# Keys and values of one attention layer projected side by side, with one context row per partition

## The chip, the cores and the metric

The kernel runs on one core of a Trainium2 chip. The metric is the device time of one execution in microseconds. A core has a matrix engine (PE, with its weight loads PEld), a vector engine (DVE), a scalar engine (ACT), a general engine (POOL), and a queue (SP) that issues the DMAs. Each engine runs its own instructions in order and waits on semaphores for the others.

## The reference

Eight stages are added to a residual `x` of 2 x 256 tokens by 512: four cross-attention layers and four small feed-forward layers. The fourth attention layer, `L3_xattn`, is the one that the change touches. It has 32 query heads in 8 groups of 4, one key and one value head of width 128 for each group, and 2 x 512 context rows:

```
q = rmsnorm(x @ Wq.T, q_norm_w)
k = rmsnorm(ctx @ Wk.T, k_norm_w)      # over the 128 values of a row; weight per value
v = ctx @ Wv.T
out = softmax(q @ k.T / sqrt(128) + mask) @ v @ Wo.T
```

Everything is float32. To keep the precision each operand is split in a high part (rounded to the matrix engine's fast float32 form) and a low part (the rest), and each product is three matmuls: high x high, high x low, low x high.

## The kernel before, in words

The four attention layers share one code (`attn_tensor`, `attn_vector`, `attn_scalar`, `attn_gpsimd`), with a table `ATTN` of what stands where. `walk` goes over the groups: two heads straight, then a loop that holds two groups in its body and starts at the third head (heads 2 and 3 of one group, heads 0 and 1 of the next, and so twice), then the rest straight. In the fourth layer the loop's body runs three times, so the loop's end is taken back twice.

A group has 4 heads and each head 4 slots, one for each tile of 128 queries. A slot is written (head, tile). In each slot the engines do the following for a tile:

- PE: `scores` of the tile two slots ahead (3 matmuls into `psS`), `transposes` of this tile's probabilities (4 into `psT`), in tiles 0 and 2 half of the weighted values (`weighted_v`, 12 matmuls of 256 columns into `psO`), in one slot of each head the query projection (12 matmuls into `psQ`), and then the units that the table `prep` or `outs` names.
- DVE: `row_max` of the tile two ahead (scale and mask L891, maximum L895), `pT_low` (L909), `row_recip` (L905), in tile 0 the low part of the output (`o_low`, L931), the low part of the query, then its share of the units.
- ACT: `pT_high`, `row_exp`, in tile 0 `o_high`, the query's high part, its share of the units, and the high parts of weights.
- POOL: `norm` (L1202), its share of the units, and the low parts of weights.

A unit uses one of two banks of `psX`, in turn. A unit may start on PE when the unit two before it has been read out, which DVE signals by `x_free`, in the order of the units. The units that `prep` names make keys and values for the next group:

- `k0`, `k1` (PE L369, 12 matmuls of 512 columns each): keys of one batch, with the 128 values of a key on the partitions and the 512 rows as columns. ACT squares them into `ksq` (L1124), DVE stores them times the norm's weight in `scr` (L966).
- `m0`, `m1` (PE L810): the sum of squares over the partitions, 4 products with a column of ones. DVE scales (L968), POOL takes the power -0.5 into `k_r` (L1219) and spreads it on diagonals (L1223).
- `b0`, `b1` (PE L814): a product of ones with these diagonals, so that every partition has every row's factor. DVE multiplies the keys by it (L970), ACT rounds them (L1131), DVE takes the low part (`k_low`, L937).
- `v0`, `v1` (PE L369, 12 matmuls of 512 columns): values in the same layout; DVE copies them to `scr` (L976). `t0`, `t1` (PE L805): 4 transposes each, since the weighted sum needs a row of values per partition. ACT rounds (L1143), DVE takes the low part (L979).
- `q` (PE L819) does for a query head what `m` does for the keys, in tile 0 of each head; DVE (L982) and POOL (L1228) follow.

`out` (PE L369, 12 matmuls of 512 columns) adds the previous group's output to `x` in slots (0,1), (0,2), (0,3) and (1,0).

## Time and profile before

| | |
|---|---|
| median of 3 runs | 2156.29 us (2155.64 to 2157.31) |
| the profiled execution, its time | 2155.29 us |
| its span, first to last instruction | 2153.5 us |
| mean granted TensorE clock | 0.968 |
| PE busy | 1971.2 us (92%) |
| PEld / DVE / ACT / POOL busy | 77% / 69% / 48% / 44% |
| chain that ended last | PE 64%, DVE 18%, ACT 9%, issue 7% |

```profile
PE   5999999999748999998988999997799999999997
DVE  5777787777777887887334555656467766677676
PEclk9999999999978999999988999999899999999999
```

These strips cut the span in 40 slices of 53.8 us; a digit is the busy share in tenths, and for the last row the granted clock. The fourth attention layer starts with a query projection at 1533 us, in slice 29, and ends at about 2120 us. The profile gives a matmul's duration with its pipeline depth, so two matmuls that follow each other overlap; what a matmul costs PE is the distance from its start to the next one's start. "[0.32 <-ACT x L1]" at a row's end is the idle time before the instruction and what ended it.

### The profile page before, as it was taken

Reading aid. Unit: us, or ns where it says so; the run is one execution under the profiler, and the core shown is the slowest. Engines: PE = TensorE matmul, PEld = TensorE weight load, DVE = VectorE, ACT = ScalarE, POOL = GpSimd, SP = SyncE. Lnnn points to the kernel's source line nnn. Section 1 sums busy time; section 2 is a strip of 40 time slices with the busy share of each in tenths; the row PEclk is TensorE's granted clock in tenths of the full one; section 3 lists DMA queues with packets and bytes.
Section 4 is the critical chain, followed back from the end, with each engine's and each line's share of the span. In section 5 each row is a group of like instructions: output and inputs, shape, how many; then the busy total and the mean of one; then the engine's idle time right before and its main releaser. Section 6 shows DMA issues by size and latency. Waiting matters only on the chain.

```text
span 2153.5 us, 33307 instructions
## 1 busy us (share of the span) xinstructions
PE 1971.2 (92%) x10874; PEld 1651.7 (77%) x10874; DVE 1475.5 (69%) x2725; ACT 1029.6 (48%) x2264; POOL 938.5 (44%) x971
## 2 busy tenths in 40 slices
PE   5999999999748999998988999997799999999997
PEld 4788888888636888887666888886678888888886
DVE  5777787777777887887334555656467766677676
ACT  3666666666514544553123544542155555545552
POOL 2555554554445665664321323322144444444432
PEclk9999999999978999999988999999899999999999
DMA  3222221122211111111210101001101110111001
GB/s 140 57 64 75 77 85 57 61 74 67 92 34 40 63 65 54 52 45 64 67 54 4 34 8 34 23 1 55 54 11 47 47 46 11 50 45 45 14 23 45
DMA packets 47070, 106.77 MB, mean 50 GB/s; under 512 B 6065, under 2 KB 21937, under 8 KB 43105
## 3 DMA queue, kind: packets, MB, share of 16 engines
q1 hardware_dynamic: 46944, 105.14, 15.3%
q8 instruction: 74, 1.21, 0.2%
q14 instruction: 52, 0.42, 0.1%
HBM read 98.37 MB, written 6.75 MB: 49 GB/s over the span
## 4 chain that ended last, share of the span: by engine, by line
PE 64%; DVE 18%; ACT 9%; issue 7%; POOL 1%; DVEq 0%; ACTq 0%; POOLq 0%
PE psX L369 23%; PE psQ L369 11%; PE psS L369 11%; PE psO L369 10%; PE psT L752 5%; DVE pT_lo L909 2%; ACT pT_hi L1092 1%; DVE dq_space L461 1%; DVE nmax L897 1%; ACT dq_space L448 1%; DVE p_sb L891 1%; DVE nbias L895 1%; PE psT L369 1%; ACT p_sb L1085 1%; DVE qscr L470 1%
## 5 line engine op out<-in xcount | busy, mean ns | idle before, releaser
L1202 POOL TENSOR_SCALAR p_sb<-p_sb,rrec 128x512 f32<-128x512 f32 (+1 forms) x320 | 266.0, 831 | 704.1 <-DVE rrec L905 704.0
L1092 ACT ACTIVATE pT_hi<-psT 128x512 fp32r<-128x512 f32 (+2 forms) x384 | 235.0, 612 | 336.9 <-PE psT L752 336.0
L909 DVE TENSOR_TENSOR pT_lo<-psT,pT_hi 128x512 fp32r<-128x512 f32 (+2 forms) x384 | 271.4, 707 | 81.9 <-ACT pT_hi L1092 81.9
L369 PE MATMUL psO<-pT_hi,v_hi 128*128 128x256 f32 (+1 forms) x832 | 255.1, 307 | 41.0 <-DVE pT_lo L909 34.1
L752 PE MATMUL psT<-ident,p_sb 128*128 128x128 f32 x1600 | 243.3, 277 | 13.9 <-POOL p_sb L1202 10.5
L369 PE MATMUL psO<-pT_hi,v_lo 128*128 128x256 f32 (+1 forms) x832 | 237.0, 285 | 0.0
L369 PE MATMUL psO<-pT_lo,v_hi 128*128 128x256 f32 (+1 forms) x832 | 237.0, 285 | 0.0
L752 PEld LDWEIGHTS psT<-ident,p_sb 128*128 128x128 f32 x1600 | 195.9, 142 | 53.1 <-POOL p_sb L1202 15.8
L369 PE MATMUL psQ<-xnT_hi,wq_hi 128*128 128x512 f32 (+1 forms) x448 | 189.0, 422 | 18.7 <-DVE qscr L869 9.2
L1085 ACT ACTIVATE p_sb<-psS,nbias 128x512 f32<-128x512 f32 (+1 forms) x192 | 145.3, 757 | 126.6 <-DVE nbias L899 126.6
L369 PEld LDWEIGHTS psO<-pT_hi,v_hi 128*128 128x128 f32 (+1 forms) x832 | 155.0, 186 | 54.2 <-DVE pT_lo L909 45.9
L369 PE MATMUL psS<-kT_hi,q_hi 128*128 128x512 f32 (+2 forms) x448 | 176.8, 395 | 20.4 <-ACT p_sb L1085 18.7
L369 PE MATMUL psQ<-xnT_hi,wq_lo 128*128 128x512 f32 (+1 forms) x448 | 180.2, 402 | 0.0
L369 PE MATMUL psQ<-xnT_lo,wq_hi 128*128 128x512 f32 (+1 forms) x448 | 179.7, 401 | 0.0
L369 PE MATMUL psX<-wo_hi,oT_hi 128*128 128x512 f32 (+1 forms) x432 | 173.1, 401 | 0.0
L369 PE MATMUL psX<-wo_hi,oT_lo 128*128 128x512 f32 (+1 forms) x432 | 169.8, 393 | 0.0
L369 PE MATMUL psX<-wo_lo,oT_hi 128*128 128x512 f32 (+1 forms) x432 | 169.5, 392 | 0.0
L624 POOL TENSOR_TENSOR wq_lo<-wq_f,wq_hi 128x512 fp32r<-128x512 f32 (+1 forms) x112 | 141.5, 1264 | 59.1 <-ACT wq_hi L612 59.1
L897 DVE TENSOR_REDUCE nmax<-psS 128x1 f32<-128x512 f32 (+1 forms) x192 | 148.1, 772 | 23.4 <-PE psS L369 23.3
L369 PE MATMUL psS<-kT_lo,q_hi 128*128 128x512 f32 (+2 forms) x448 | 163.6, 365 | 0.0
L369 PE MATMUL psS<-kT_hi,q_lo 128*128 128x512 f32 (+2 forms) x448 | 163.3, 364 | 0.0
L369 PE MATMUL psX<-cT_hi,wkv_hi 128*128 128x512 f32 (+1 forms) x384 | 157.6, 410 | 0.8 <-DVE q_ms L982 0.2
(337 smaller groups left out, 4786.2 us busy)
## 6 DMA issues: line engine op xcount, KB each, us to landing
wq_f<-in_a_wq SPq DMA_DIRECT2D x96, 256.0 KB, 2.7
wo_f<-in_a_wo SPq DMA_DIRECT2D x24, 1024.0 KB, 6.1
wkv_f<-in_a_wkv SPq DMA_DIRECT2D x24, 512.0 KB, 3.9
mask_sb<-in_codes SPq DMA_DIRECT2D x32, 174.0 KB, 2.4
qscr<-in_amax SPq DMA_DIRECT2D x32, 174.0 KB, 2.3
w<-qscr SPq DMA_DIRECT2D x32, 174.0 KB, 1.9
wo_f<-in_f_wT SPq DMA_DIRECT2D x3, 1024.0 KB, 5.2
wq_f<-in_a_wq SPq DMA_DIRECT2D x16, 192.0 KB, 2.3
```

Of the source, the lines that this page charges most:

```text
L369: mm = pe.matmul(dst, w, m, start=(first and k == 0), stop=(last and k == n - 1))
L448: ins = act.activation(tiles[q], dq_codes[h % 2], ACT.Copy, scale=slope, bias=NF4[c] - slope * c)
L461: dve.tensor_tensor(t[0], t[0], t[2], ALU.min).then_inc(dq_low, 1)
L470: dve.tensor_tensor(t[0], t[0], t[2], ALU.max).then_inc(dq_high, 1)
L624: L.wq_lo.inc(pool.tensor_tensor(lo, f, hi.bitcast(F32), ALU.subtract))
L752: mm = pe.transpose(t_view(L, j)[:, i, :], p_view(L, j, h)[:, m * P:(m + 1) * P], ident[:, :])
L891: L.s_mask.inc(dve.scalar_tensor_tensor(p_view(L, j), s_view(L, j)[:, 0:L.open(j)], scale, mask_sb[:, t * L.keys:t * L.keys + L.open(j)], ...
L897: L.s_nm.inc(dve.tensor_reduce(nmax[:, j:j + 1], s_view(L, j), AX.X, ALU.max, negate=True))
L909: L.t_lo.inc(dve.tensor_tensor(pT_view(L, pT_lo, j), t_view(L, j), pT_view(L, pT_hi, j).bitcast(F32), ALU.subtract))
L1085: L.s_exp.inc(act.activation(p_view(L, j), src, ACT.Exp, bias=nbias[:, j:j + 1], scale=1.0 if L.masked else L.scale, accum_out=rsum[:, j:j ...
L1092: L.t_hi.inc(act.activation(pT_view(L, pT_hi, j), t_view(L, j), ACT.Copy))
L1202: L.s_norm.inc(pool.tensor_scalar(p_view(L, j), p_view(L, j), rrec[:, j:j + 1], 1.0, ALU.mult, ALU.mult))
```

## The change

In the fourth layer the weights of keys and values are interleaved in memory, so that for each 128 inputs 128 columns of keys and 128 of values lie side by side (`wkv_rows`). The context is now the stationary operand and the weights are streamed. The units of the layer become:

- `n0` to `n3`: each takes two tiles of 128 context rows. PE does 24 matmuls of 256 columns; a bank holds two halves of 128 key values and 128 values, with a context row per partition. ACT squares the two key tiles with the sum accumulated in the same instruction (into `k_ms`), then writes `v_hi`. DVE writes `v_lo`. POOL does a small scaling and the power -0.5 on 2 columns (L1246, L1248 of the changed kernel). DVE multiplies the keys by the factor into `scr` (`k_scale`), and only this frees the bank.
- `k0`, `k1`: 4 transposes each of these keys. ACT and DVE write the high and low parts with the norm's weight, straight from `psX`.

`m`, `b`, `v`, `t` and `k_low` are gone. `k_scale` of a unit stands on DVE in the slot after the unit's, behind `row_max`, `pT_low`, `row_recip` and `o_low`; for `n0` in slot (1,3), the last before the loop's end, it stands at the end of the same slot. `k0` is behind `n1` and `k1` behind `n3` by an explicit wait, and every unit is behind the unit two before it.

```diff
          outs=OUT_EARLY, splits=SPLIT_TILES,
-         prep={(1, 3): ["k0"], (2, 0): ["k1", "m0"], (2, 1): ["m1"], (2, 2): ["b0"], (2, 3): ["v0", "b1"],
-               (3, 0): ["t0"], (3, 1): ["v1"], (3, 2): ["t1"]}),
+         prep={(1, 3): ["n0"], (2, 2): ["n1"], (2, 3): ["n2"], (3, 0): ["k0"], (3, 1): ["n3"], (3, 2): ["k1"]}),
...
-        diag = rows[:, :].rearrange("p (a b) -> p a b", b=P)
+        ksq_tiles = ksq[:, :, :].rearrange("p a (t d) -> p (a t) d", d=P)
+        kn = scr[:, :, :].rearrange("p a (t d) -> p (a t) d", d=P)
+        wkv_rows = [z[:, :, :].rearrange("p a (c n) -> p (a c) n", n=2 * P) for z in (wkv_hi, wkv_lo)]
...
                     if h == 0:
-                        if L.masked:
+                        if L.rope:
                             L.k_lo.wait(pe, g.at(L.n_k, L.n_k))
-                        else:
+                        elif not L.rms:
                             prev = g.to(-1) if g.off else None
                             L.x_free.wait(pe, L.use(prev, f"k{L.n_k - 1}")[0] + 1)
+                if L.rms and h == 0 and j in (0, 2):
+                    prev = g.to(-1) if g.off else None
+                    L.x_free.wait(pe, L.use(prev, f"k{b}")[0] + 1)
...
+                elif kind == "n":
+                    L.wkv_lo.wait(pe, gp.at(2, 2))
+                    for z in (0, 1):
+                        at = (2 * i + z) * P
+                        mm = three(pe, X[:, z * 2 * P:(z + 1) * 2 * P],
+                                   [([m[:, c, at:at + P] for m in (cT_hi, cT_lo)], [w[:, c, :] for w in wkv_rows])
+                                    for c in range(DC)])
+                elif kind == "k" and L.rms:
+                    L.x_free.wait(pe, L.use(g, f"n{2 * i + 1}")[0] + 1)
+                    for m in range(4):
+                        mm = pe.transpose(X[:, m * P:(m + 1) * P], kn[:, 4 * i + m, :], ident[:, :])
...
-                elif kind == "m":
-                    L.k_f.wait(pe, L.count(g, "k", f"k{i}"))
-                    for m in range(4):
-                        mm = pe.matmul(X[:, m:m + 1], ksq[:, i, m * P:(m + 1) * P], ones[:, 0:1],
-                                       start=True, stop=True)
-                elif kind == "b":
-                    L.k_diag.wait(pe, L.count(g, "b", what))
-                    mm = pe.matmul(X, ones[:, :], diag[:, :, :].rearrange("p a b -> p (a b)"), start=True, stop=True)
...
-                    ins = dve.tensor_scalar(scr[:, i, :], X, vecs[:, 1:2], None, ALU.mult)
-                elif kind == "m":
-                    ins = dve.tensor_scalar(k_ms[:, i, :], X[:, 0:4], 1.0 / hd, EPS, ALU.mult, ALU.add)
-                elif kind == "b":
-                    ins = dve.tensor_tensor(scr[:, i, :], scr[:, i, :], X, ALU.mult)
-                    late.append((g, i, kpar))
+                    ins = dve.scalar_tensor_tensor(k_lo, X, vecs[:, 1:2], k_hi.bitcast(F32), ALU.mult, ALU.subtract)
+                elif kind == "n":
+                    c = slice(2 * i * P, 2 * (i + 1) * P)
+                    dve.tensor_tensor(v_lo[:, kpar, c].rearrange("p (t d) -> p t d", d=P), halves(X)[:, :, P:2 * P],
+                                      v_hi[:, kpar, c].bitcast(F32).rearrange("p (t d) -> p t d", d=P), ALU.subtract)
+                    late.append((g, what, X))
+                    return
...
+            def k_scale(g, what, X):
+                i = int(what[1])
+                L.k_r.wait(dve, 2 * (i + 1) if g is None else g.at(8, 8 + 2 * (i + 1)))
+                L.x_free.inc(dve.tensor_tensor(kn[:, 2 * i:2 * i + 2, :], halves(X)[:, :, 0:P],
+                                               k_r[:, i // 2, 2 * (i % 2):2 * (i % 2) + 2].unsqueeze(2).broadcast_to([P, 2, P]),
+                                               ALU.mult))
...
+                    while L.rms and late:
+                        k_scale(*late.pop(0))
...
-                    while late and late[0] in before:
-                        k_low(*late.pop(0))
+                    while L.rms and late and (h, j) == (1, 3):
+                        k_scale(*late.pop(0))
...
-                if kind == "k" and L.rms:
+                if kind == "n":
                     L.x_mm.wait(act, k + 1)
-                    L.k_f.inc(act.activation(ksq[:, i, :], X, ACT.Square))
-                elif (kind == "k" and L.rope) or kind == "b":
-
-                    if L.rope:
-                        L.k_f.wait(act, L.count(g, "k", what))
-                    else:
-                        L.x_free.wait(act, k + 1)
+                    for z in (0, 1):
+                        t = 2 * i + z
+                        ins = act.activation(ksq_tiles[:, t, :], halves(X)[:, z, 0:P], ACT.Square,
+                                             accum_out=k_ms[:, t // 4, t % 4:t % 4 + 1])
+                    L.k_sq.inc(ins)
+                    c = slice(2 * i * P, 2 * (i + 1) * P)
+                    L.x_act.inc(act.activation(v_hi[:, gp.par, c].rearrange("p (t d) -> p t d", d=P),
+                                               halves(X)[:, :, P:2 * P], ACT.Copy))
...
+                    elif L.rms:
+                        ins = act.activation(dst, X, ACT.Copy, scale=vecs[:, 1:2])
...
-                elif what[0] == "m":
+                elif what[0] == "n":
                     i = int(what[1])
-                    L.x_free.wait(pool, k + 1)
-                    L.k_r.inc(pool.tensor_tensor(k_r[:, i, :], k_ms[:, i, :], half[:, 0:4], ALU.pow))
-                    L.k_r.wait(pool, L.count(g, "m", what))
-                    if i:
-                        L.x_mm.wait(pool, L.use(g, "b0")[0] + 1)
-                    L.k_diag.inc(pool.tensor_tensor(diag[:, :, :], ident[:, :].unsqueeze(1).broadcast_to([P, 4, P]),
-                                                    k_r[:, i, :].unsqueeze(2).broadcast_to([P, 4, P]), ALU.mult))
+                    at = (slice(None), i // 2, slice(2 * (i % 2), 2 * (i % 2) + 2))
+                    L.k_sq.wait(pool, i + 1 if g is None else g.at(4, 4 + i + 1))
+                    pool.sem_inc(wait_met, 1)
+                    L.k_r.inc(pool.tensor_scalar(k_ms[at], k_ms[at], 1.0 / L.hd, EPS, ALU.mult, ALU.add))
+                    L.k_r.wait(pool, 2 * i + 1 if g is None else g.at(8, 8 + 2 * i + 1))
+                    L.k_r.inc(pool.tensor_tensor(k_r[at], k_ms[at], half[:, 0:2], ALU.pow))
...
-        k, v = (split(w, n).reshape(n, P, DC * hd) for w in (wk, wv))
-        arrays[f"a{i}_wkv"] = np.stack([k, v], axis=2)
+        k, v = (split(w, n).reshape(n, P, DC, hd) for w in (wk, wv))
+        arrays[f"a{i}_wkv"] = np.stack([k, v], axis=3 if i == 3 else 2).reshape(n, P, 2, DC * hd)
```

On DVE, at slot (3,0), from its `row_max` on, before (L891 mask, L895 maximum, L909 `pT_low`, L905 `row_recip`, L931 `o_low`, L982 and L979 the reads of `q` and `t0`, L937 `k_low`):

```order
L891 SCALAR_TENSOR_TENSOR p_sb<-psS,q_r,mask_sb 128x512
L125 REGISTER_ALU
L895 TENSOR_REDUCE nbias<-p_sb 128x1
L909 TENSOR_TENSOR pT_lo<-psT,pT_hi 128x4x128
L905 RECIPROCAL rrec<-rsum 128x1
L125 REGISTER_ALU
L931 TENSOR_TENSOR oT_lo<-psO,oT_hi 128x512
L125 REGISTER_ALU
L982 TENSOR_SCALAR q_ms<-psX 128x4
L125 REGISTER_ALU
L979 TENSOR_TENSOR v_lo<-psX,v_hi 128x512
L937 TENSOR_TENSOR kT_lo<-scr,kT_hi 128x512
```

and after, one `v_lo` (L977, of `n2`) earlier (L902, L906, L920, L916 and L942 are the same five steps, L997 is `k_scale`):

```order
L977 TENSOR_TENSOR v_lo<-psX,v_hi 128x256
L124 REGISTER_ALU
L902 SCALAR_TENSOR_TENSOR p_sb<-psS,q_r,mask_sb 128x512
L124 REGISTER_ALU
L906 TENSOR_REDUCE nbias<-p_sb 128x1
L920 TENSOR_TENSOR pT_lo<-psT,pT_hi 128x4x128
L916 RECIPROCAL rrec<-rsum 128x1
L124 REGISTER_ALU
L942 TENSOR_TENSOR oT_lo<-psO,oT_hi 128x512
L124 REGISTER_ALU
L997 TENSOR_TENSOR scr<-psX,k_r 128x256
L124 REGISTER_ALU
```

The bank of `n2` is freed by the row L997, which stands behind the five steps; `k0` on PE needs that bank.

On DVE, at slot (3,2), the same; before, from the end of slot (3,1), with the copy of `v1` (L976) that frees its bank ahead of the next `row_max`:

```order
L905 RECIPROCAL rrec<-rsum 128x1
L125 REGISTER_ALU
L976 COPY scr<-psX 128x512
L125 REGISTER_ALU x2
L891 SCALAR_TENSOR_TENSOR p_sb<-psS,q_r,mask_sb 128x512
L125 REGISTER_ALU
L895 TENSOR_REDUCE nbias<-p_sb 128x1
L909 TENSOR_TENSOR pT_lo<-psT,pT_hi 128x4x128
L905 RECIPROCAL rrec<-rsum 128x1
L125 REGISTER_ALU
L979 TENSOR_TENSOR v_lo<-psX,v_hi 128x512
```

and after, from the read of `n3` (L977) on:

```order
L977 TENSOR_TENSOR v_lo<-psX,v_hi 128x256
L124 REGISTER_ALU x2
L902 SCALAR_TENSOR_TENSOR p_sb<-psS,q_r,mask_sb 128x512
L124 REGISTER_ALU
L906 TENSOR_REDUCE nbias<-p_sb 128x1
L920 TENSOR_TENSOR pT_lo<-psT,pT_hi 128x4x128
L916 RECIPROCAL rrec<-rsum 128x1
L124 REGISTER_ALU
L997 TENSOR_TENSOR scr<-psX,k_r 128x256
L124 REGISTER_ALU
L974 SCALAR_TENSOR_TENSOR kT_lo<-psX,vecs,kT_hi 128x512
```

The row that frees `n3` moved from ahead of the four steps of slot (3,2) to behind them; PE's `k1` is in this slot.

On PE, at the end of slot (2,1), before:

```order
L369 MATMUL psQ<-xnT_lo,wq_hi 128x512
L125 REGISTER_ALU x2
L810 MATMUL psX<-ones,xn_f 128x1 x4
L125 REGISTER_ALU
L369 MATMUL psS<-kT_hi,q_hi 128x512
L369 MATMUL psS<-kT_hi,q_lo 128x512
L369 MATMUL psS<-kT_lo,q_hi 128x512
```

and after:

```order
L371 MATMUL psQ<-xnT_lo,wq_hi 128x512
L124 REGISTER_ALU
L371 MATMUL psS<-kT_hi,q_hi 128x512
L371 MATMUL psS<-kT_hi,q_lo 128x512
L371 MATMUL psS<-kT_lo,q_hi 128x512
```

The sum over partitions is gone, and `psS` follows the projection directly.

## Rows read from the trace of the kernel before

**Rows 1.** First line of the page.
```profile
span 2153.5 us, 33307 instructions
```

**Rows 2.** Busy time by stretch, fourth layer's loop: start:end, length, engines, clock, DMA, GB/s.
```profile
1600.00:2080.00 480.00, 476.12 (x2767) 407.45 (x2766) 340.05 (x620) 244.97 (x508) 216.12 (x228) 1.00 0.12 37
```

**Rows 3.** PE in time, end of `m0`: start, us, engine, line, work.
```profile
1672.57 0.95 PE L810 MATMUL psX<-ones,xn_f 128*128 128x1 f32 x8
...
1673.38 0.49 PE L369 MATMUL psS<-kT_hi,q_hi 128*128 128x512 f32 x1
...
1673.71 0.40 PE L369 MATMUL psS<-kT_hi,q_lo 128*128 128x512 f32 x1
```

**Rows 4.** PE in time, around `b0`.
```profile
1680.82 1.02 PE L814 MATMUL psX<-rows,ones 128*128 128x512 f32 x2
...
1681.28 0.79 PE L369 MATMUL psS<-kT_hi,q_hi 128*128 128x512 f32 x1
...
1681.91 0.39 PE L369 MATMUL psS<-kT_hi,q_lo 128*128 128x512 f32 x1
```

**Rows 5.** Chain of waits, one projection unit: start, us, what.
```profile
1663.76 2.77 PE psX L369 x12
```

**Rows 6.** Groups by form, PE, 1600 to 2080 us: busy us, mean ns, idle before.
```profile
L810 PE MATMUL psX<-ones,xn_f 128*128 128x1 f32 x112 | 13.4, 241 | 3.2 <-DVE q_ms L982 3.2
...
L805 PE MATMUL psX<-ident,scr 128*128 128x128 f32 x56 | 8.6, 277 | 0.0
```

**Rows 7.** PE in time, slot (3,2) from its scores to `t1`.
```profile
1694.51 0.39 PE L369 MATMUL psS<-kT_hi,q_hi 128*128 128x512 f32 x1
...
1695.75 0.28 PE L369 MATMUL psO<-pT_hi,v_lo 128*128 128x256 f32 x1
...
1697.05 0.60 PE L805 MATMUL psX<-ident,scr 128*128 128x128 f32 x4
```

**Rows 8.** DVE in time, steps of slots (3,0) and (3,1).
```profile
1690.35 0.16 DVE L905 RECIPROCAL rrec<-rsum 128x1 f32<-128x1 f32 x1 [0.28 <-ACT p_sb L1085]
...
1690.83 0.69 DVE L931 TENSOR_TENSOR oT_lo<-psO,oT_hi 128x512 fp32r<-128x512 f32 x1 [0.32 <-ACT oT_hi L1114]
...
1693.04 0.75 DVE L891 SCALAR_TENSOR_TENSOR p_sb<-psS,q_r,mask_sb 128x512 f32<-128x512 f32 x1
...
1695.39 0.16 DVE L905 RECIPROCAL rrec<-rsum 128x1 f32<-128x1 f32 x1 [0.29 <-ACT p_sb L1085]
```

**Rows 9.** Groups by form, ACT, whole run.
```profile
L1081 ACT ACTIVATE p_sb<-p_sb,nbias 128x128 f32<-128x128 f32 x64 | 25.7, 402 | 81.4 <-DVE nbias L885 81.4
...
L1085 ACT ACTIVATION_READ_ACCUMULATOR p_sb<-p_sb,nbias 128x1 f32 x128 | 23.8, 186 | 0.0
```

**Rows 10.** Groups by form, DVE, whole run: a 128x256 product.
```profile
L1594 DVE TENSOR_TENSOR xn_f<-xn_f 128x256 f32<-128x256 f32 x1 | 0.4, 426 | 0.0
```

**Rows 11.** Groups by form, POOL, whole run.
```profile
L1219 POOL TENSOR_TENSOR k_r<-k_ms,half 128x4 f32<-128x4 f32 x16 | 16.2, 1013 | 26.2 <-DVE k_ms L968 26.2
```

**Rows 12.** DVE in time, across the loop's end.
```profile
1738.05 0.75 DVE L966 TENSOR_SCALAR scr<-psX,vecs 128x512 f32<-128x512 f32 x1 [0.32 <-ACT xn_f L1124]
...
1741.44 0.75 DVE L891 SCALAR_TENSOR_TENSOR p_sb<-psS,q_r,mask_sb 128x512 f32<-128x512 f32 x1 [2.63 <-issue]
...
1744.88 0.15 DVE L982 TENSOR_SCALAR q_ms<-psX 128x4 f32<-128x4 f32 x1
```

**Rows 13.** PE in time, `m0` after the loop's end.
```profile
1745.16 1.05 PE L810 MATMUL psX<-ones,xn_f 128*128 128x1 f32 x8 [1.39 <-DVE q_ms L982]
```

**Rows 14.** PE in time, start of the layer: first `k0`, then the second query projection.
```profile
1537.51 0.39 PE L369 MATMUL psX<-cT_hi,wkv_hi 128*128 128x512 f32 x1
...
1559.23 0.48 PE L369 MATMUL psQ<-xnT_hi,wq_hi 128*128 128x512 f32 x1
```

**Rows 15.** PE in time, a wait near the end of the third layer.
```profile
1433.97 0.63 PE L369 MATMUL psS<-kT_hi,q_hi 96*128 96x512 f32 x1 [2.43 <-ACT p_sb L1085]
```

**Rows 16.** Busy time by stretch, after that wait.
```profile
1433.00:1440.00 7.00, 6.03 (x33) 5.66 (x34) 3.07 (x6) 3.13 (x6) 2.64 (x3) 0.76 0.00 0
```

More of the change, by code:

```diff
@@ L371, in three, with halves @@
             return mm
+        def halves(bank):
+            return bank.rearrange("p (t n) -> p t n", n=2 * P)
         def flat(t):
@@ L1029, in head @@
                         row_recip(*settled)
-                    before = list(late)
                     while L.rope and late:
@@ L1209, in use @@
             def use(g, what):
-                if what[0] not in "kmq" or what[0] == "out":
+                if what[0] not in "knq" or what[0] == "out":
                     return
```

30 lines of the change are left out of this document (16 added, 14 removed).

## The prediction

> **What bounds the kernel now.** I read the page's span first [rows 1], then the busy time by stretch: over 480 us of the fourth layer's loop PE is busy 476 us at granted clock 1.00, that is at 2.4 GHz, and DVE, ACT and POOL are busy 71%, 51% and 45% [rows 2]. So in this layer time is PE's work plus the little it waits. Then I read PE in order of time, because a matmul's duration overlaps the next; only distances between starts count. Last I read DVE in order of time, since DVE frees the banks that PE's units wait for. PE never waited for the value transposes `t` (idle 0.0) and 3.2 us in all for `m` [rows 6], the whole of it after the loop's end. The group row also gives the count: 112 records at 8 for each `m` are 14 units, two for each of the 7 groups that prepare a next one.
>
> **PE's work.** A unit `m` takes 0.81 us from its start to the scores behind it, and the first matmul of these takes 0.33 us instead of 0.23, because it follows work in the other float form [rows 3]: 0.91 us. A unit `b` takes 0.46 us, and the matmul behind it 0.63 instead of 0.23 [rows 4]: 0.86 us. Two of each go: 3.54 us for a group. A `k` or `v` unit of 12 matmuls of 512 columns takes 2.77 us [rows 5]; the weighted values show what 256 columns with a weight load each cost, 11 in 1.30 us, 0.118 us each [rows 7]. An `n` unit of 24 is then 2.84 us, and four cost 0.28 us more than the four units that they replace. The new `k` transposes are as many as the `t` ones were, in the same slots, so they cancel. Net -3.26 us for a group, -22.8 us for 7.
>
> **A wait that the change adds at `k1`.** I count from the start of slot (3,2) on PE, which is the end of `n3`. PE reaches the transposes after 1697.05 - 1694.51 = 2.54 us [rows 7]. `k1` needs `k_scale` of `n3`. Before that, ACT squares two tiles of 128 columns, each with the read of its sum. Nothing shows this form; the nearest is an exponential of 128 columns at 0.40 us with a read of 0.19 us behind it [rows 9]. An activation starts about 0.1 us before the last one's end, so that two squares hold ACT 0.8 us by this row; from below I put 0.55 us, an estimate, a third less for a form that takes no bias operand. Copying the values to `v_hi` takes 0.4 to 0.5 us (the same row's 0.40 us is for half the columns). With 0.2 us until the last product has landed and a semaphore passed, DVE can start on `v_lo` at 1.2 to 1.5 us, and holds 0.35 us for it (a 128x256 product lasts 0.43 us [rows 10]). Then `row_max`, the maximum, `pT_low` and the reciprocal stand in front: from a mask's start to a reciprocal's start 1695.39 - 1693.04 = 2.35 us, and 0.16 us for it [rows 8]. Then `k_scale`, 0.43 us. The sum is 4.5 to 4.8 us against PE's 2.54: a wait of 2.0 to 2.3 us. I take 2.2. Behind it on PE's queue stand the scores of the next head and the query projection, so it is paid in full.
>
> **And at `k0`.** In slot (3,0) PE does scores, transposes, half of the weighted values and the `q` unit, 3.4 us: the 2.54 us above holds the first three, and the `q` sum is as long as an `m`, 0.81 us. `k0` follows `n2` by two units and needs its bank. DVE's chain is the same, with `o_low` in it, which starts 1690.83 - 1690.35 = 0.48 us after the reciprocal and holds DVE 0.6 us [rows 8]. `k_scale` ends at 5.5 to 5.8 us: a wait of 2.1 to 2.4 us. I take 2.3. The two waits are 4.5 us for a group and 31.5 us for 7, more than PE's saved work. As ends for the pair I keep 2.8 us for a group (each square nearly free, and `v_lo` let through before ACT has finished other work) and 5.5 us (the new small instructions are as long as their nearest rows).
>
> **POOL and the loop's end.** POOL's scaling of 2 columns has no row; the power on 4 columns lasts 1.01 us [rows 11]. I take 0.35 us and 0.9 us, with 0.1 us and 1.0 us as the ends for the first. This is hidden where `k_scale` stands a slot later, since the factor is there before DVE comes to it. In slot (1,3) it isn't hidden: `k_scale` of `n0` stands at the slot's end and waits for POOL. There DVE's last instruction started at 1738.05, 0.75 us after PE's slot, and the loop's end cost 3.39 us from there to the next one [rows 12]. Now the last is `k_scale`, which starts after squares (0.9 us), scaling and power and POOL's `norm` before them, at about 2.6 us. DVE enters the loop's body 1.9 us later than before, near 1743.3 on the old time axis. PE has lost its `m` and `k1` units in (2,0) and (2,1), so it comes early: it waits about 1.4 us at the transposes of slot (2,2), whose probabilities come from that late `row_max`, and 1.8 us more at the weighted values behind them, which need `pT_low` of slot (2,1), itself behind the `q_ms` that was at 1744.88 [rows 12]. In place of this, the old wait of 1.39 us at `m0` [rows 13] goes. Net +1.6 us, twice: +3.2 us. In the groups without a loop's end a small part of this remains, some 0.3 us in 5 groups, +1.5 us.
>
> **The layer's start.** From the first key unit to the second query projection it was 1559.23 - 1537.51 = 21.7 us [rows 14], with waits and a lowered clock in it. The new chain is: `n0` and `n1` 5.7 us, `n2` to 8.8, `k0` to 9.2, a wait for `n2` to be read until 11.8, `n3` to 14.6, a wait of 3 us, `k1` and `q` to 18.8. That is 2.9 us less, and the two waits of nearly 3 us will cost part of it by the clock: I take -1 us, between -3 and +2.
>
> **Clock.** After a wait of 2.43 us [rows 15] seven microseconds had a mean clock of 0.76 [rows 16], with part of the stretch at 1.2 GHz; 0.24 x 7 = 1.7 us were lost. Behind the 1.39 us of [rows 13] the loop's mean of 1.00 [rows 2] shows no such loss. The new waits of 2.2 us lie between. I put one fall, +2 us, in the sum. The Trainium skill, "TensorE: Matmul & The Clock Gate", section "HAM oscillation — how this bites in real kernels", says that the array's clock is halved again after idle gaps, and that a kernel with such a gap in each tile pays each time. By that rule the sum would be that of the second rival below. The trace agrees for one gap of 2.43 us and shows none for the short ones.
>
> **Sum.** -22.8 + 31.5 + 3.2 + 1.5 - 1 + 2 = +14.4 us on the profiled execution's 2155.3 us (its span of 2153.5 and 1.8 us around it) gives 2169.7. The median is 1.0 us above that execution: 2170.7, so I say 2171 us.
>
> **Rivals.**
> 1. Faster: the waits don't appear, because DVE, idle 29% of the loop [rows 2], runs far enough ahead of PE that each bank is free in time. For it speaks that `t` never waited [rows 6]; against it, that the copy which freed `v1` stood ahead of `row_max`, and `k_scale` stands behind it, and that the scores of this `row_max` are themselves made by PE at the slot's start, so DVE can't run ahead. Then 2156.3 - 22.8, and 2.9 us less at the start: 2131 us. It decides if the waits of a group stay below 3.3 us.
> 2. Slower still: the clock falls at most of the 14 long waits. For it [rows 15, 16], against it the short stretch of each wait. 10 falls at 1.7 us instead of 1: 2171 + 15 = 2186 us.
> 3. No change: the mechanism holds, but both waits are near their low end, 2.8 us for a group: 12 us less, 2159 us.
> 4. The weight loads of the `n` units don't hide behind 256 columns, so that each matmul takes as long as one weight load. The loop's loads are 407.45 / 2766 = 0.147 us long on average [rows 2]; 96 matmuls at that instead of 0.118 us are 2.8 us for a group, and 2171 + 8 x 2.8 = 2193 us. The weighted values do the same pattern at 0.118 us [rows 7], so I hardly believe it.
>
> **How the numbers follow.** The forecast has 0.60, the faster rival 0.11, the clock 0.14, no change 0.12, weight loads 0.03. The point is the forecast's. The forecast's own range, from waits of 3.5 to 5.3 us for a group and the start's bounds, is 2162 to 2179 us. The range 2151 to 2187 us takes in the third rival and the second, and leaves out the first and the fourth and the ends, about 0.2. What a measurement of this kernel can tell from no change is about 0.2%, 4.3 us: faster 0.11, within it 0.13, slower 0.76.
>
> **What would show it.** In the changed kernel's groups of work: no `m` or `b`; `n` matmuls 0.118 us apart; PE idle before the transposes of `scr` of about 4.5 us for a group, with DVE's `scr` as releaser, split evenly on `k0` and `k1`; PE waits at `psT` and `psO` just behind the loop's end; a loop body of two groups 2 x (4.5 - 3.26) + 0.3 + 1.6 = 4.4 us longer than before. If the transposes show idle under 3 us for a group, my chain on DVE is wrong; if the `n` matmuls are further apart than 0.13 us, the PE term is.

## The result

| | median | runs |
|---|---|---|
| before | 2156.80 us | 4 (2155.64 to 2158.45) |
| after | 2168.69 us | 4 (2166.28 to 2171.01) |

The ratio is 1.0056, with a 95% interval from 1.0041 to 1.0070: the change makes the kernel 12 us slower. The profiled execution of after took 2167.1 us, 11.8 us more than that of before.

### The profile page after: what moved, and what is told of

It reads as the page before. It is cut to its first block, busy times and chain, and to the rows that moved or that the text cites. A ratio compares the mean times of both kernels' runs of the same rounds, so it can differ in the third digit from the quotient of the medians.

```text
span 2165.3 us, 33868 instructions
## 1 busy us (share of the span) xinstructions
PE 1956.6 (90%) x11098; PEld 1660.2 (77%) x11098; DVE 1451.2 (67%) x2709; ACT 1042.6 (48%) x2392; POOL 933.5 (43%) x1003
## 4 chain that ended last, share of the span: by engine, by line
PE 63%; DVE 17%; ACT 9%; issue 7%; POOL 1%; DVEq 0%; ACTq 0%; POOLq 0%
PE psX L371 24%; PE psQ L371 11%; PE psS L371 10%; PE psO L371 9%; PE psT L760 5%; DVE pT_lo L920 2%; ACT pT_hi L1111 1%; DVE dq_space L466 1%; ACT dq_space L453 1%; DVE nmax L908 1%; DVE p_sb L902 1%; ACT p_sb L1104 1%; PE psT L371 1%; DVE nbias L906 1%; DVE qscr L475 1%
## 5 line engine op out<-in xcount | busy, mean ns | idle before, releaser
L920 DVE TENSOR_TENSOR pT_lo<-psT,pT_hi 128x512 fp32r<-128x512 f32 (+2 forms) x384 | 271.1, 706 | 82.3 <-ACT pT_hi L1111 82.3
L371 PE MATMUL psS<-kT_hi,q_hi 128*128 128x512 f32 (+2 forms) x448 | 171.0, 382 | 24.3 <-ACT p_sb L1104 18.7
L1104 ACT ACTIVATE p_sb<-p_sb,nbias 128x512 f32<-128x512 f32 x128 | 92.6, 724 | 136.2 <-DVE nbias L906 136.1
```

Of the source, the lines that this page charges most:

```text
L371: mm = pe.matmul(dst, w, m, start=(first and k == 0), stop=(last and k == n - 1))
L920: L.t_lo.inc(dve.tensor_tensor(pT_view(L, pT_lo, j), t_view(L, j), pT_view(L, pT_hi, j).bitcast(F32), ALU.subtract))
L1104: L.s_exp.inc(act.activation(p_view(L, j), src, ACT.Exp, bias=nbias[:, j:j + 1], scale=1.0 if L.masked else L.scale, accum_out=rsum[:, j:j ...
```

## The profile after

The first line of the page, against [rows 1]:

```profile
span 2165.3 us, 33868 instructions
```

The busy time of the loop's stretch (start:end, length, then PE, PEld, DVE, ACT, POOL, the granted clock, the share of the DMA engines and GB/s), against [rows 2]:

```profile
1600.00:2080.00 480.00, 449.69 (x2890) 402.30 (x2891) 313.08 (x596) 253.57 (x611) 206.92 (x252) 0.99 0.12 37
```

PE is busy 449.69 us of 480, where it was 476.12. DVE and POOL are less busy than before, and ACT only 9 us more, so no engine took PE's place as the bound. PE waits. For what, the groups by form show (busy us, mean ns, idle before), against [rows 6]:

```profile
L371 PE MATMUL psX<-wkv_hi,cT_hi 128*128 128x256 f32 x216 | 63.6, 294 | 0.0
L371 PE MATMUL psO<-pT_hi,v_hi 128*128 128x256 f32 x208 | 62.4, 300 | 1.6 <-DVE pT_lo L920 1.6
...
L806 PE MATMUL psX<-ident,scr 128*128 128x128 f32 x56 | 10.1, 307 | 24.8 <-DVE scr L997 24.8
```

L806 are the transposes of `k0` and `k1`: 24.8 us of idle time, all released by DVE's `scr`, the result of `k_scale`. 56 records at 4 for each unit are 14 units. In the order of time each `k0` waits 1.86 or 1.87 us and each `k1` 1.66 to 1.68 us (1.73 once, in the last group). Here is PE in slot (3,2) of one group, in the order of time, with what stood there before in [rows 7]:

```profile
1843.81 0.40 PE L371 MATMUL psS<-kT_hi,q_hi 128*128 128x512 f32 x1
...
1846.25 0.28 PE L371 MATMUL psO<-pT_lo,v_hi 128*128 128x256 f32 x1
1848.20 0.66 PE L806 MATMUL psX<-ident,scr 128*128 128x128 f32 x4 [1.68 <-DVE scr L997]
```

And DVE in the same slot, against [rows 8]:

```profile
1844.94 0.42 DVE L977 TENSOR_TENSOR v_lo<-psX,v_hi 128x256 fp32r<-128x256 f32 x1 [1.04 <-ACT v_hi L1149]
1845.28 0.74 DVE L902 SCALAR_TENSOR_TENSOR p_sb<-psS,q_r,mask_sb 128x512 f32<-128x512 f32 x1
1846.06 0.69 DVE L906 TENSOR_REDUCE nbias<-p_sb 128x1 f32<-128x512 f32 x1
1846.66 0.68 DVE L920 TENSOR_TENSOR pT_lo<-psT,pT_hi 128x512 fp32r<-128x512 f32 x1
1847.62 0.16 DVE L916 RECIPROCAL rrec<-rsum 128x1 f32<-128x1 f32 x1 [0.29 <-ACT p_sb L1104]
1847.72 0.42 DVE L997 TENSOR_TENSOR scr<-psX,k_r 128x256 f32<-128x256 f32 x1
```

From the mask step (L902) to `k_scale` (L997) it is 2.44 us from start to start, in which DVE waits for ACT (0.29 us on the reciprocal), and the transposes on PE begin 0.06 us after the end of `k_scale`. ACT, which starts the chain, was quicker than predicted; the same view of ACT, against [rows 9]:

```profile
1844.01 0.28 ACT L1145 ACTIVATE xn_f<-psX 128x128 f32<-128x128 f32 x1 [0.30 <-PE psX L371]
1844.18 0.20 ACT L1145 ACTIVATION_READ_ACCUMULATOR xn_f<-psX 128x1 f32 x1
1844.27 0.27 ACT L1145 ACTIVATE xn_f<-psX 128x128 f32<-128x128 f32 x1
1844.43 0.20 ACT L1145 ACTIVATION_READ_ACCUMULATOR xn_f<-psX 128x1 f32 x1
1844.52 0.38 ACT L1149 ACTIVATE v_hi<-psX 128x256 fp32r<-128x256 f32 x1
```

The two squares with their reads hold ACT from 1844.01 to 1844.52, 0.51 us. POOL's two instructions, groups by form over 1600 to 2080 us, against [rows 11]:

```profile
L1248 POOL TENSOR_TENSOR k_r<-k_ms,half 128x2 f32<-128x2 f32 x27 | 19.0, 703 | 2.2
...
L1246 POOL TENSOR_SCALAR k_ms<-k_ms 128x2 f32<-128x2 f32 x27 | 5.2, 193 | 6.2 <-ACT xn_f L1145 3.7
```

At the loop's end, PE in the order of time (the last matmul of `n0`, then the next scores):

```profile
1742.25 0.28 PE L371 MATMUL psX<-wkv_lo,cT_hi 128*128 128x256 f32 x1
1744.45 0.49 PE L371 MATMUL psS<-kT_hi,q_hi 128*128 128x512 f32 x1 [1.92 <-issue]
1744.78 0.40 PE L371 MATMUL psS<-kT_hi,q_lo 128*128 128x512 f32 x1
```

and DVE, against [rows 12]:

```profile
1743.49 0.42 DVE L977 TENSOR_TENSOR v_lo<-psX,v_hi 128x256 fp32r<-128x256 f32 x1 [0.63 <-ACT v_hi L1149]
1744.86 0.42 DVE L997 TENSOR_TENSOR scr<-psX,k_r 128x256 f32<-128x256 f32 x1 [0.94 <-POOL k_r L1248]
1748.44 0.75 DVE L902 SCALAR_TENSOR_TENSOR p_sb<-psS,q_r,mask_sb 128x512 f32<-128x512 f32 x1 [3.15 <-issue]
```

PE itself waits for nothing that the profile shows ("issue") for 1.92 us; at the other pass of the loop's end it is 1.91 us. Before, PE had no such gap there. DVE's `k_scale` waits 0.94 us for POOL and its next instruction comes 3.58 us after it.

A useful yardstick is the distance from the start of one group's first `out` matmul to that of the next (PE, `psX<-wo_hi,oT_hi`). The loop's end is in the second and in the fourth distance:

| kernel | first mark | distances of the 7 groups, us |
|---|---|---|
| before | 1637.93 | 70.78, 72.70, 70.78, 72.88, 70.79, 70.84, 54.40 |
| after | 1640.93 | 72.90, 74.69, 71.38, 75.89, 71.38, 71.38, 54.58 |

A steady group (no loop's end, no fall of the clock) is 0.60 us longer. 72.90 and 75.89 hold a fall of the clock, shown below.

## The experiments

Theory A: the change did cut PE's work, and the loss is one queue position on DVE. `k_scale` stands behind `pT_low`, the reciprocal and `o_low`, each of which needs a result of ACT first, and PE's `k0` and `k1` wait for it. The rivals: the chain that makes the factor (squares, POOL) is itself too long, or DVE is late as a whole, so that a wait taken from one place comes back at another. Theory C is on PE's idle time at the loop's end, which the prediction had not foreseen: it would be PE's jump back, hidden before the change behind queued matmuls of 512 columns, which last twice as long as those of 256. Its rival D: the idle time comes from the changed loop body itself, its length or its place. The kernels e1 to e4 ran in one session and e5 to e8 in another, on another chip, and each ratio is to runs of the kernel before made in the same session. e3 and e4 were run once each, so their times have no interval.

| kernel | median, us | ratio to before, 95% |
|---|---|---|
| e1 `k_scale` early in all slots | 2141.78 | 0.9928 [0.9913, 0.9943] |
| e2 early in (3,2) alone, for `k1` | 2158.00 | 1.0008 [0.9994, 1.0021] |
| e3 before, `k0` in (1,2) | 2173.92, one run | |
| e4 after, query projection last before the loop's end | 2170.76, one run | |
| e5 e1 and e4 together | 2136.83 | 0.9910 [0.9893, 0.9927] |
| e6 early in (3,0) alone, for `k0` | 2152.39 | 0.9981 [0.9972, 0.9991] |
| e7 one step later than e1 | 2142.30 | 0.9938 [0.9922, 0.9955] |
| e8 e1 with `n0` in (1,2) | 2149.66 | 0.9969 [0.9958, 0.9980] |

**e1: `k_scale` between the mask step and the maximum.**

```diff
             late = []
+            between = []
...
                                                           ALU.mult, ALU.add))
+                    while between and between[0] and late:
+                        k_scale(*late.pop(0))
                     L.s_mask.wait(dve, g.at(L.group_slots, k + 1))
...
                     nxt = L.step(g, h, j, L.ahead)
+                    between[:] = [L.rms and True]
                     if nxt:
                         row_max(*nxt)
+                    between[:] = []
```

> The changed kernel with one thing moved on the vector engine: the product that scales the keys and frees the bank of an n unit stands between the mask step and the maximum of row_max in the next slot, instead of behind pT_low, the reciprocal and o_low. Theory A (the added waits come from the place of this product in the vector engine's order): PE's waits at the k transposes fall from 1.86 and 1.68 us to under 0.5 us each, the clock no longer falls at them, the two-group loop body goes from 146.1 to about 139.5 us, and the time is 2140 us (2135 to 2147). Rival B (the waits come from the longer chain through ScalarE and GpSimd, squares, sum, power, so the factor is late wherever the product stands): the waits stay above 1.3 us, the product now delays the maximum too, and the time is 2165 us or more.

Measured: 2141.78 us, 27 us less than after and 15 us less than before, inside theory A's range; the loop's body took 139.27 us, where 139.5 was expected, and the clock fell in none of the groups. PE's groups by form over the same stretch:

```profile
L371 PE MATMUL psS<-kT_hi,q_hi 128*128 128x512 f32 x112 | 47.2, 421 | 3.6 <-issue 3.6
...
L806 PE MATMUL psX<-ident,scr 128*128 128x128 f32 x56 | 9.0, 284 | 0.0
```

The 24.8 us are 0.0, and 3.6 us of issue at the loop's end stay. PE is busy 472 us of the stretch's 480 again, nearly as before the change, but with less work in each group:

```profile
1600.00:2080.00 480.00, 472.21 (x3050) 421.08 (x3048) 329.23 (x628) 260.57 (x633) 214.93 (x261) 1.00 0.12 37
```

DVE and PE in slot (3,2), one after the other (here L980 is `v_lo`, L903 the mask step, L1000 `k_scale`, L909 the maximum):

```profile
1831.61 0.42 DVE L980 TENSOR_TENSOR v_lo<-psX,v_hi 128x256 fp32r<-128x256 f32 x1 [1.08 <-ACT v_hi L1154]
1831.95 0.74 DVE L903 SCALAR_TENSOR_TENSOR p_sb<-psS,q_r,mask_sb 128x512 f32<-128x512 f32 x1
1832.61 0.41 DVE L1000 TENSOR_TENSOR scr<-psX,k_r 128x256 f32<-128x256 f32 x1
1832.94 0.68 DVE L909 TENSOR_REDUCE nbias<-p_sb 128x1 f32<-128x512 f32 x1
```

```profile
1830.47 0.40 PE L371 MATMUL psS<-kT_hi,q_hi 128*128 128x512 f32 x1
...
1833.08 0.66 PE L806 MATMUL psX<-ident,scr 128*128 128x128 f32 x4
```

`k_scale` ends at 1833.02, 2.55 us after PE's slot began at 1830.47, and PE is there at 1833.08: just in time. No wait for POOL is shown on L1000, so the chain that makes the factor doesn't bind, though by little: POOL's power ran from 1831.78 to 1832.48, and `k_scale` started at 1832.61. The distances are 68.06, 71.20, 68.07, 70.84, 68.05, 68.12, 54.02. With 0.24 us of waiting in such a group (ahead of `n3`, for DVE's read of the `q` unit), and 3.54 in after's, after's 71.38 should be 68.06 + 3.54 - 0.24 = 71.36. So the two waits are the whole difference between the kernels in a steady group.

**e2: the same move only in slot (3,2), so only for `k1`.** The diff is e1's, with

```diff
-                    between[:] = [L.rms and True]
+                    between[:] = [L.rms and (h, j) == (3, 2)]
```

> The same move, but only in slot (3,2), where it frees n3 for k1; k0 keeps its wait. Theory A: the wait at k1 goes, the one at k0 stays at 1.9 us, a loop body is 3.7 us shorter: 2168.7 - 7 x 1.8 = 2156 us if the clock still falls three times at k0, 2152 if it takes both gaps to make it fall. Rival B: k1 keeps more than 1 us of wait, 2163 us or more.

Measured: 2158.00 us. The waits on PE (us in total, times, longest), over 1600 to 2080 us:

```profile
PE psX L806 <- DVE scr L1000: 13.1, 7, 1.9
```

`k1`'s wait is gone and `k0`'s is untouched at 1.87 us, 7 times. The distances are 69.58, 74.52, 71.10, 72.51, 71.13, 71.16, 55.21. A group without a fall of the clock is 69.58, 1.80 us less than after's. But 71.10 is one with a fall, and there are 5 of these where after has 3. So 7 x 1.8 = 12.6 us went and 2 x 1.5 = 3 us came: 9.6 us, and 10.7 us were measured between the medians. The number of falls is that of one profiled execution: the 12 runs of e2 go from 2153.0 to 2167.8 us, and the longer ones have the lower mean granted clock (0.964 down to 0.957).

**e6: the move only in slot (3,0), so only for `k0`.** The same line, with `(h, j) == (3, 0)`.

> k_scale behind the mask step in slot (3,0) alone, so that only k0 is served early. Theory A (the place of k_scale on DVE makes each wait by itself): the 1.87 us ahead of k0 go in all 7 groups, and the wait of 1.67 us ahead of k1 stays in all 7: 7 x 1.87 = 13 us less than 2168, and without the clock's falls, which came behind k0's wait, 4.6 us less again: 2151 us (2148 to 2154). If the shorter wait at k1 makes the clock fall as k0's did (1.5 us each), as moving only k1 left falls behind k0, 3 falls give 2155, 7 falls 2161. Rival (DVE is late as a whole): the wait at k1 grows by about what k0 loses, and the time stays within 4 us of 2168.

Measured: 2152.39 us, as theory A has it. The waits on PE, same view:

```profile
PE psX L806 <- DVE scr L1000: 11.8, 7, 1.7
```

`k1` waits 1.68 us, no more than in after, and the only wait that came in place of `k0`'s is one of 0.18 us ahead of `n3`. A steady group is 69.78 us, 1.60 less than after's. 1.60 and 1.80 add up to 3.40, and both moves at once (e1) gave 71.38 - 68.06 = 3.32, so the two waits are nearly independent of each other. And no group of e6 has a fall of the clock.

**e7: one step later on DVE, behind the maximum.** The diff is against e1.

```diff
-                    while between and between[0] and late:
-                        k_scale(*late.pop(0))
                     L.s_mask.wait(dve, g.at(L.group_slots, k + 1))
                     L.s_max.inc(dve.tensor_reduce(nbias[:, j:j + 1], p_view(L, j), AX.X, ALU.max, negate=True))
+                    while between and between[0] and late:
+                        k_scale(*late.pop(0))
```

> k_scale one step later in all slots: behind the maximum of row_max, still ahead of pT_low, the reciprocal and o_low. Theory A counts DVE's steps: k_scale comes 0.7 us later than behind the mask step, against the 2.1 us (k1) and 3.2 us (k0) by which the steps ahead of it were cut; by that PE waits 0 to 0.3 us at k0 or n3 and 0.8 us at k1 in each group, some 7 us more than the 2142 us of the mask place, from which the maximum, and with it the exponential, gains back about 0: 2148 us (2144 to 2152). Rival: only being ahead of pT_low matters, since that step waits for ACT: then 2142 us, with no wait at k1.

Measured: 2142.30 us, which by the total is the rival's number. The groups speak for A: `k1` waits 0.60 us in each (0.69 in the last, 4.3 us in all), `k0` not at all, and the distances are 68.50, 71.99, 68.52, 71.24, 68.48, 68.57, 54.00, in sum 2.9 us more than e1's. In 71.99 the clock fell once, behind PE's idle time of 1.76 us at the loop's end.

```profile
L806 PE MATMUL psX<-ident,scr 128*128 128x128 f32 x56 | 9.0, 284 | 4.3 <-DVE scr L1000 4.3
```

Between the two profiled executions this does not show in the total because the first mark stands at 1634.73 here and at 1637.45 in e1. The first query projection of the layer starts at 1532.29 in the one profile and at 1535.39 in the other, so these 3 us come from the code ahead of the layer, which is the same in both. My 7 us were too many: the wait is 0.60 instead of 0.8 us, and that of `k0` or `n3` isn't there.

**e4: after, with the query projection of head 1 last before the loop's end.**

```diff
-         groups=8, keys=512, slots=4, nbuf=2, ahead=2, settle=2, q_slot=(1, 1, 1, 3),
+         groups=8, keys=512, slots=4, nbuf=2, ahead=2, settle=2, q_slot=(1, 3, 1, 3),
...
-         prep={(1, 3): ["n0"], (2, 2): ["n1"],
+         prep={(1, 1): ["n0"], (2, 2): ["n1"],
```

> The changed kernel with the query projection of head 1 in slot (1,3), just ahead of the loop's end, and n0 in (1,1). Theory C: the 1.92 us of issue at PE's scores behind the loop's end go, since 12 matmuls of 512 columns stand ahead of it; but PE then reaches the transposes and weighted values of slot (2,2) earlier and waits there for the vector engine 2 us more than now, so the time is within 4 us of 2168. Rival D: the issue idle stays at 1.9 us and the time is 2170 or more.

Measured: 2170.76 us. PE's idle time without a releaser at the loop's end fell from 1.92 and 1.91 us to 0.18 and 0.37 us, and the wait at `psO` behind it grew to 1.48 and 1.09 us. Rival D had the idle time stay.

**e5: e1 and e4 together.**

> The kernel with k_scale behind the mask step, and in addition the query projection of head 1 in slot (1,3), just ahead of the loop's end, with n0 in slot (1,1). Theory: PE's idle time at the loop's end is its jump, hidden behind the matmuls that are already queued, and these last twice as long with 512 columns as with 256. Then PE's issue idle of 1.61 and 1.95 us goes to 0.4 us or less at both ends; the wait at psO behind it grows by up to 1 us each. 2139 us in all (2135 to 2142) against 2142. Rival: the idle time has another cause at that place; then it stays at 1.6 to 2.0 us, and the time at 2142 or above.

Measured: 2136.83 us, the lowest median, 0.9% less than before; its interval overlaps that of e1. PE at the loop's end, the last two matmuls of the projection and the next scores:

```profile
1732.84 0.39 PE L371 MATMUL psQ<-xnT_hi,wq_lo 128*128 128x512 f32 x1
1733.07 0.39 PE L371 MATMUL psQ<-xnT_lo,wq_hi 128*128 128x512 f32 x1
1733.53 0.49 PE L371 MATMUL psS<-kT_hi,q_hi 128*128 128x512 f32 x1
```

1733.53 - 1733.07 = 0.46 us where one such matmul follows another in 0.23: 0.2 us of idle time, against 1.61 us at this place in e1:

```profile
1733.92 0.28 PE L371 MATMUL psX<-wkv_lo,cT_hi 128*128 128x256 f32 x1
1735.81 0.49 PE L371 MATMUL psS<-kT_hi,q_hi 128*128 128x512 f32 x1 [1.61 <-issue]
```

So the gap is there or not by how long the work ahead of the loop's end lasts. The distances of e5 are 68.35, 70.18, 68.36, 70.14, 68.36, 68.42, 54.12: a loop's end costs 1.8 us more than a steady group instead of 3.14 and 2.78, but each steady group is 0.3 us longer. In sum this is 467.93 us against e1's 468.36. Of the 5 us between the medians the layer's loop explains half a microsecond. The rest is ahead of the first mark (1635.99 against 1637.45) and elsewhere, and I can't say that it is the edit's.

**e3: the kernel before, with `k0` one slot earlier.**

```diff
-         prep={(1, 3): ["k0"], (2, 0): ["k1", "m0"],
+         prep={(1, 2): ["k0"], (2, 0): ["k1", "m0"],
```

> The kernel before with the unit k0 in slot (1,2) instead of (1,3), so that no projection of 512 columns stands on PE just ahead of the loop's end. Theory C (PE's own jump at the loop's end takes some 3 us, and was hidden by the long 512-column matmuls queued ahead of it; 256-column ones leave no such lead, so 1.92 us show in the changed kernel): PE now shows an idle time ended by issue at the scores behind the loop's end, 1.5 to 2.5 us, twice. Rival D (the idle is a matter of the changed loop body, its length or place in memory): none shows, and the vector engine's 2.6 us stays the only one. Time about 2157 to 2161.

Measured: 2173.92 us, 17 us more than before, and not for the expected reason. The 1.5 to 2.5 us of idle time that theory C forecast did not come: PE stood 0.19 us at one loop's end and not at all at the other. Between `k0` and the loop's end there were still three scores of 512 columns and four transposes, and the paragraph on PE's jump at the end shows that they were enough. Instead a wait at `psO` came up in each of the 7 groups, 1.17 to 1.20 us and once 0.76. DVE's read of `k0` (L966) waits 1.54 us for ACT's square, and `pT_low` stands behind it in DVE's queue:

```profile
1669.26 0.75 DVE L966 TENSOR_SCALAR scr<-psX,vecs 128x512 f32<-128x512 f32 x1 [1.54 <-ACT xn_f L1124]
...
1671.31 0.68 DVE L909 TENSOR_TENSOR pT_lo<-psT,pT_hi 128x512 fp32r<-128x512 f32 x1
```

A steady group took 72.22 us. Behind the loop's two ends the waits at `m0` were 2.13 and 1.93 us, and the clock fell behind both. The expectation, made from the loop's end alone, missed all of this.

**e8: e1 with `n0` in (1,2), the counterpart of e3 with 256 columns.**

```diff
-         prep={(1, 3): ["n0"], (2, 2): ["n1"],
+         prep={(1, 2): ["n0"], (2, 2): ["n1"],
```

> k_scale behind the mask step, and n0 moved from slot (1,3) to (1,2), so that 3 products of 512 columns and 4 transposes stand between n0 and the loop's end. It is the counterpart of the kernel before with k0 in (1,2), where PE had no idle time at the loop's end. If the jump is hidden behind what PE has queued, and the queue holds some 16 matmuls, then 9 of them are now of 256 columns instead of 512, cover 1 us less, and PE idles 0.5 to 1.5 us at issue at both ends, between the 0 of that kernel and the 1.6 to 2.0 of n0 in (1,3). If instead only the unit that stands last counts, it idles 0.2 us or less. In time a new wait at psO appears in every group, as in that kernel (1.2 us): 2142 + 7 x 1.5 - 2 = 2150 us (2144 to 2158).

Measured: 2149.66 us, as expected. The new wait at `psO` came in five of the 7 groups (1.35 to 1.50 us); in the two with a loop's end PE stands at the scores instead:

```profile
1735.35 0.60 PE L760 MATMUL psT<-ident,p_sb 128*128 128x128 f32 x4
1737.51 0.49 PE L371 MATMUL psS<-kT_hi,q_hi 128*128 128x512 f32 x1 [1.55 <-DVE p_sb L903]
```

PE did idle 1.55 us (1.14 at the other end), near the 0.5 to 1.5 us that were expected, but the row names DVE's mask step, which ended at 1736.87, as the releaser. DVE was late because its `v_lo` of `n0` waited 1.97 us for ACT. So up to 1736.87 PE would have waited in any case. But PE went on only 0.64 us after that end, where `k1`'s transposes in after followed `k_scale` by 0.06 us, so at this end something else came last; the paragraph on PE's jump shows what. At the other end DVE's step ended at 1878.07 and PE went on at 1878.29.

## Why the prediction was right

The forecast was 2171 us, and 2168.69 was measured. The mechanism held: PE's work fell, and two waits for `k_scale` gave back more. Term by term, on the profiled execution:

| term | predicted, us | measured, us |
|---|---|---|
| PE's work, 7 groups | -22.8 | -20.6 |
| waits at `k0` and `k1` | +31.5 | +24.8 |
| loop's end, twice | +3.2 | +2.3 |
| small waits in 5 groups | +1.5 | 0 |
| the layer's start | -1 | -0.7 |
| falls of the clock | +2 | +4.6 |
| ahead of the layer | 0 | +1.0 |
| sum | +14.4 | +11.4 |

The execution itself was 11.8 us longer.

That the forecast came within 2.3 us is in part luck. The waits were put 6.7 us too high, the term of the sum that was most off, and 3.54 us for a group is the low end of the 3.5 to 5.3 us that the prediction gave its own range. With the loop's end and the small waits, 9.1 us were put too high. Three terms that came out higher than predicted, the falls of the clock (+2.6 us), PE's work (+2.2 us) and the code ahead of the layer (+1.0 us), took 5.8 us of this back. The loop's body of two groups, forecast 4.4 us longer, was 2.6 us longer (143.48 to 146.07 us).

**PE's work.** A steady group less its waits is 71.38 - 3.54 = 67.84 us, against 70.78 with no wait before: -2.94 us, and 7 times this is -20.6. I had -3.26. A part of the missing 0.32 us is the spacing of the `n` matmuls, which is 0.120 us and not the 0.118 us read from [rows 7]: 96 x 0.002 = 0.19 us. The prediction put the late second score behind an `m` unit (0.33 us instead of 0.23) down to the other float form. In after the same 0.33 us stands behind the idle time at the loop's end (1744.45 to 1744.78), where `n0` in the fast form came before, so the form alone isn't shown to be its cause. The `n` units never waited for their weights (the fourth rival): their groups show no idle time, and 24 of them take 2.86 us.

**The waits.** This is the term that was too large: 3.54 us for a group against 4.5. From the start of slot (3,2), `k_scale` ended after 4.33 us (1843.81 to 1848.14) where I had 4.5 to 4.8. In it the steps of DVE from the mask to the reciprocal were 2.34 us against 2.35 predicted from [rows 8]. What was too long is the part that no row showed: two squares held ACT 0.51 us, and I had 0.55 to 0.8. PE's side was too short by the same kind of detail: it came free at 1846.52, 2.71 us after the slot began, because a wait is counted from the modelled end of the last matmul, not from the point where the next one could have started (2.54). For `k0` it is the same: its slot began at 1833.93, `k_scale` ended at 1839.25, so 5.32 us against the 5.5 to 5.8 predicted, PE came free at 1837.45, 3.52 us against 3.4, and the wait is 1.86 us against 2.3. The claim that the two waits are paid in full, since the next head's scores stand behind them, is what e2, e6 and e1 show: without them a group is shorter by 1.80, 1.60 and 3.32 us.

**The loop's end.** The size was about right and the place was wrong. I expected waits at `psT` and `psO` of 1.4 and 1.8 us (less the old wait of 1.39 us this is 1.8 and not the 1.6 of the sum, which comes out with the mean of both old waits, 3.2 / 2 us). The one at `psT` didn't come; the one at `psO` was 0.98 and 0.65 us. DVE was late as forecast: it entered the loop's body 6.07 us after PE had issued the last of `n0` (1742.37 to 1748.44), 1.9 us more than the same stretch before, 1741.44 - (1738.05 - 0.75) = 4.14 us by [rows 12]. But PE was late too, by its own idle time of 1.92 us, which I hadn't in the sum, and this took the place of a part of the wait for DVE. In e4, where this idle time was gone, the wait at `psO` grew by 0.5 and 0.4 us. By the marks, the two ends cost 74.69 - 71.38 = 3.31 and 75.89 - 71.38 - 1.52 = 2.99 us more than a steady group, against 1.92 and 2.10 before: +2.3 us. The 0.3 us that I put in five other groups weren't there: a steady group has no other idle time on PE than the 3.54 us.

**The start.** From the first unit to the second query projection:

```profile
1538.72 0.28 PE L371 MATMUL psX<-wkv_hi,cT_hi 128*128 128x256 f32 x1
...
1549.87 0.39 PE L371 MATMUL psX<-wkv_hi,cT_hi 128*128 128x256 f32 x1 [1.91 <-DVE scr L997]
...
1555.43 1.09 PE L806 MATMUL psX<-ident,scr 128*128 128x128 f32 x4 [2.43 <-DVE scr L997]
...
1557.88 0.77 PE L371 MATMUL psQ<-xnT_hi,wq_hi 128*128 128x512 f32 x1
```

19.16 us against the 21.72 of [rows 14], with the two waits and the slow clock that were foreseen (the transposes at 1555.43 take 1.09 us instead of 0.66). The projection behind them then ran at 1.2 GHz for the most part and took 4.69 us from its start to the scores behind it (1562.57), where it was 2.85 (1559.23 to 1562.08), which leaves -0.7 us.

**The clock.** I put one fall in the sum, and there were three, behind `k0`'s waits. Two groups' transposes for comparison:

```profile
1691.71 1.12 PE L806 MATMUL psX<-ident,scr 128*128 128x128 f32 x4 [1.86 <-DVE scr L997]
...
1839.31 0.66 PE L806 MATMUL psX<-ident,scr 128*128 128x128 f32 x4 [1.86 <-DVE scr L997]
```

After the same wait of 1.86 us the transposes took 1.12 us in one group, at 1.2 GHz, and 0.66 in the other, at 2.4. The busy time by stretch, as in [rows 16]:

```profile
1691.00:1698.00 7.00, 6.29 (x37) 5.86 (x38) 3.59 (x8) 2.16 (x5) 1.92 (x3) 0.76 0.34 136
1839.00:1846.00 7.00, 6.69 (x51) 6.34 (x52) 4.24 (x9) 3.60 (x10) 2.60 (x4) 1.00 0.32 133
```

The granted clock is 0.76 in the one and 1.00 in the other. From `k0` to `k1` it is 10.43 us with a fall and 8.89 without: 1.5 us each. In the prediction I cited the Trainium skill, "TensorE: Matmul & The Clock Gate", section "HAM oscillation — how this bites in real kernels", for a kernel that pays in each tile. The gaps in the page's kernel are waits for a DMA and longer than any wait in this layer's loop, and the rule as I used it, a fall behind each gap, did not hold in after. The clock fell behind 3 of after's 7 long waits, so the second rival (10 falls) was not the case; e2 came nearer to it with 5 of 7.

**The rivals.** The faster one (no waits, 2131 us) needs `k_scale` ahead of `pT_low`: this is what e1 built, and it measured 2141.78, not 2131. A steady group of e1 is 2.72 us shorter than before's and not 3.26, which is 3.8 us over 7 groups; its two loop's ends cost 1.9 us more than before's; the layer's start gained 0.7 us and not 2.9; and in the profiled execution the code ahead of the layer took 2.4 us longer, which the edit doesn't touch. No change (2159 us) needed waits of 2.8 us for a group: 3.54 lies between it and my 4.5.

## What to carry to other kernels

Where an engine in order frees a buffer, what counts is what stands ahead of the freeing instruction in its queue, above all steps that wait for a third engine: moving one product of 0.42 us ahead of three or four steps, most of which wait for ACT, turned a change that cost 12 us into one that gains 15. DVE was idle a third of the time, yet its order set PE's waits. e3 is a second case: there it was `pT_low` that stood behind a step waiting for ACT. Before a change that puts a new reader in front of a buffer's release is judged, count from the producer's end to the release on the reader's queue, and compare that with what the producer's engine still has to do; in e1, e2, e6 and e7 the waits moved as that difference did.
